# Three attention loops on one core: TensorE's step in a new order, with the product with V right behind the scores

## The chip, the core and the metric

The kernel runs on one core of a Trainium2 chip. The metric is device time in microseconds (us) of one execution, the median of several. The core's engines are TensorE (PE in the rows, with PEld for its weight loads, which overlap its matmuls), VectorE (DVE), ScalarE (ACT), GpSimd (POOL) and SyncE (SP). Each runs its own list of instructions in order, and they meet through semaphores.

## What is computed

The input is x, 128 sequences of 64 tokens with 128 features, and a context of the same shape. Eight layers follow each other, four attentions and four feed-forward layers, each added to x. The change touches the function that computes the attentions of layer 0 (L0a: a mask for each query and key), layer 1 (L1a: a mask for each key, and a relative bias) and the last layer, which the reference calls a feed-forward layer but which is an attention as well (L3f: no mask, projections mixed from four experts for each sequence). In short:

```
for each sequence (64 tokens, 16 heads of 8):
    xhat = layernorm(x)                      # L3f: scaled in the same way
    q = xhat @ Wq; k = ctx @ Wk; v = ctx @ Wv      # L3f: all three from xhat, weights mixed per sequence
    s = q k' * scale + bias (L1a);  s = masked (L0a, L1a)
    p = softmax(s);  o = p @ v
    x = x + o @ Wo + bo
```

## The kernel before

Function `attention` (line 270 on) works on 64 tiles of 128 tokens, two sequences a tile. It is one software pipeline: at step i each engine does, for several tiles at once, one piece each, and `at(i, r, lag)` names tile u = i - lag and its slot s. The order in which these pieces are written out for an engine is the order in which it does them. TensorE's pieces of a step, in the order before the change:

- V (lag 4, lines 464 and 469): the context or xT times Wv, into the bank psQKV.
- masks and scores (lag 4, lines 481 to 500): the relative bias (481, L1a), the masks (493 in tiles of 32x32 of the array in L0a, 488 in L1a), then the scores, 16 matmuls in tiles of 32x64 (500), into psS. They wait for wide_made (GpSimd's product of K with the pattern of heads, line 409).
- TY (lag 1, line 509): the transpose of xhat, into psTY.
- oT (lag 7, line 512): the transpose of the normalised output On, into psO.
- PT0 (lag 5, line 448): four transposes of the first half of the subtracted scores, into psPT.
- QK (lag 2, lines 531 and 533, in L3f 527 with eight matmuls): Q and K, into psQKV.
- O (lag 6, line 543): the exponentials times V, 64 matmuls in tiles of 128x32, into psO.
- Y (lag 7, line 552): oT times Wo, into psTY.
- PT1 (lag 5, line 448): the second four transposes, into psPT again. They wait for pt0_kept, ScalarE's exp that reads the first half.

A float32 matmul here is two instructions, so QK has four loads, V two and Y two; a transpose is one.

ScalarE's pieces, before the change: copy V to Vblk (578 or 583, lag 4); L3f: half of the mixed weights (590); copy oT (597, 601 or 604, lag 7); copy xT (609, lag 1; VectorE does it in L3f, 668); exp of the first half (614, lag 5); copy Q to still and K to flat (624 and 626, 631 and 632, or 634 and 635, lag 2); L3f: the other half of the weights (638); exp of the second half (642, lag 5); L3f: xhat (646).

VectorE's pieces: maximum of the scores (659, lag 4); L3f: copy xT (668); subtraction of the maximum, "less" (674, lag 4); L3f: mixed weights (681); reciprocal and On (690 and 692, lag 6); sum into x (699, lag 7); statistics (703).

Two waits matter. Before V, TensorE waits for `qk_kept` to reach u + 2, which is flat of tile i - 3, copied in ScalarE's step i - 1 (V, Q and K share the bank psQKV); where there are masks, it waits there for `less_made` too, the subtraction of the tile before. That one protects psS, which the masks overwrite:

```python
for u, s in at(i, r, 4):
    wait(pe, qk_kept, u + 2, NT)
    wait(pe, v_kept, u)
    if masked:
        wait(pe, mask_made, u + 1)
        wait(pe, less_made, u)
```

Of the kernel before, what the change touches and what calls it, by code (L numbers as in the profile page):

```python
# [17 lines left out]
P = 128  # L18
# [242 lines left out]
def attention(c, name, sems, w, mask=None, key_mask=False, rel=None, scale=1.0, ctxT=None, q_bias=None, k_bias=None,  # L261
# [6 lines left out]
    with ExitStack() as ctx:  # L268
# [60 lines left out]
        def at(i, r, lag):  # L329

            u = i - lag
            if not isinstance(u, int) or 0 <= u < NT:
                yield u, (r - lag) % RING
# [110 lines left out]
        def _(pe):  # L444
# [7 lines left out]
            def step(i, r):  # L452
# [4 lines left out]
                for u, s in at(i, r, 4):  # L457
                    wait(pe, qk_kept, u + 2, NT)
                    wait(pe, v_kept, u)
                    if masked:  # L460
                        wait(pe, mask_made, u + 1)
                        wait(pe, less_made, u)
                    if not moe:
                        mm = pe.matmul(psQKV[:, 256:384], ctx_sb[:, s, :], w["v"][:, 0, :], start=True, stop=True,
                                       skip_group_check=True)
                    else:
                        for b in range(B2):
                            for h in range(2):
                                mm = pe.matmul(psQKV[S * h:S * h + S, 256 + S * b:256 + S * b + S].rearrange(  # L469
                                    "p (g d) -> p g d", d=DH), xT[:, s, b * S:b * S + S],  # L470
                                               Wc[:, s, b, 2 * P:3 * P].rearrange(
                                                   "k (g h d) -> k g h d", g=8, h=2)[:, :, h, :],
                                               start=b == 0, stop=True, skip_group_check=True)
                    mm.then_inc(v_done, 1)
                for u, s in at(i, r, 4):

                    if not masked:
                        wait(pe, less_made, u)
                    if rel is not None:
                        for g in range(4):  # L480
                            pe.matmul(psS[:, g, 0:256], rel["flip"][:, :],
# [16 lines left out]
                    for g in range(4):  # L498
                        for b in range(B2):
# [2 lines left out]
                                           wide[32 * g:32 * g + 32, s, b].rearrange("p j n -> p (j n)"),  # L502
                                           start=not masked, stop=True, skip_group_check=True)
                    mm.then_inc(s_done, 1)
                for u, s in at(i, r, 1):
                    wait(pe, xhat_made, u + 1)
                    wait(pe, xT_kept, u)
                    wait(pe, x_summed, u - 6)
                    pe.transpose(psTY[:, 0:P], xhat[:, s, :], c.ident[:, :]).then_inc(xT_done, 1)
                for u, s in at(i, r, 7):  # L510
                    wait(pe, on_made, u + 1)
                    pe.transpose(psO[:, ON:ON + P], On[:, s, :], c.ident[:, :]).then_inc(oT_done, 1)  # L512
                for u, s in at(i, r, 5):
                    wait(pe, less_made, u + 1)
                    wait(pe, pt1_kept, u)
                    transposed(u, s, 0).then_inc(pt0_done, 1)
                for u, s in at(i, r, 2):
                    wait(pe, xT_kept, u + 1)
                    wait(pe, qk_kept, u)
# [13 lines left out]
                        mm = pe.matmul(psQKV[:, P:2 * P], w["k"][:, 0, :], ctx_sb[:, s, :], start=False, stop=True,  # L533
                                       skip_group_check=True)
                    mm.then_inc(qk_done, 1)
                for u, s in at(i, r, 6):
                    wait(pe, oT_kept, u)
                    wait(pe, v_kept, u + 1)
                    wait(pe, pt1_kept, u + 1)
                    for gj in range(8):  # L540
                        for q in (0, 2, 1, 3):
                            rows = slice(32 * q, 32 * q + 32)
                            mm = pe.matmul(psO[rows, 18 * gj:18 * gj + 18], PT[:, s % 2, gj, rows],  # L543
                                           Vb[:, s, q // 2, gj].rearrange("p h d -> p (h d)"),
                                           start=gj == 0, stop=True, skip_group_check=True,
                                           tile_position=(0, 32 * q))
                    mm.then_inc(o_done, 1)
                for u, s in at(i, r, 7):
                    wait(pe, oT_kept, u + 1)
                    wait(pe, xT_kept, u + 7, NT)  # L550
                    wait(pe, x_summed, u)
                    pe.matmul(psTY[:, Y:Y + P], oT[:, s, :], w["o"][:, :], start=True, stop=True,  # L552
                              skip_group_check=True).then_inc(y_done, 1)
                for u, s in at(i, r, 5):
                    wait(pe, pt0_kept, u + 1)
                    transposed(u, s, 1).then_inc(pt1_done, 1)
            run_steps(pe, NT, DEPTH, RING, step)

        @block.scalar
        def _(act):  # L560
# [3 lines left out]
            def step(i, r):  # L564
# [22 lines left out]
                if moe:  # L587
                    for u, s in at(i, r, 0):
                        wait(act, wc_made, u - 3)
                        act.activation(Wa[:, s, 0, :], w_all[:, bass.ds(first_at[0], 3 * P)], ACT.Copy,  # L590
                                       scale=moe["two"][:, 0, bass.ds(B2 * u, 1)])
                for u, s in at(i, r, 7):
                    wait(act, oT_done, u + 1)
                    wait(act, y_done, u - 3)
                    if moe:
                        for b in range(B2):
                            last = act.activation(oT[:, s, S * b:S * b + S], psO[:, ON + S * b:ON + S * b + S],  # L597
                                                  ACT.Identity, bias=moe["v_bias"][:, bass.ds(B2 * u + b, 1)])
                        last.then_inc(oT_kept, 1)
                    elif v_bias_col is not None:  # L600
                        act.activation(oT[:, s, :], psO[:, ON:ON + P], ACT.Identity, bias=v_bias_col
                                       ).then_inc(oT_kept, 1)
                    else:
                        act.activation(oT[:, s, :], psO[:, ON:ON + P], ACT.Copy).then_inc(oT_kept, 1)
                if not moe:
                    for u, s in at(i, r, 1):
                        wait(act, xT_done, u + 1)
                        wait(act, qk_done, u - 3)
                        act.activation(xT[:, s, :], psTY[:, 0:P], ACT.Copy).then_inc(xT_kept, 1)
                for u, s in at(i, r, 5):  # L610

                    wait(act, o_done, u - 1)
                    wait(act, pt0_done, u + 1)
                    act.activation(PT[:, s % 2, 0:4, :].rearrange("p g n -> p (g n)"), psPT[:, :], ACT.Exp  # L614
                                   ).then_inc(pt0_kept, 1)
                for u, s in at(i, r, 2):
                    wait(act, qk_done, u + 1)
                    wait(act, s_done, u - 3)
# [32 lines left out]
        def _(dve):  # L651
# [3 lines left out]
            def step(i, r):  # L655
# [29 lines left out]
                        last.then_inc(wc_made, 1)  # L685
                for u, s in at(i, r, 6):
                    wait(dve, o_done, u + 1)
                    wait(dve, oT_done, u - 3)
                    Ov = psO[:, 0:144].rearrange("p (h d) -> p h d", d=DH + 1)
                    dve.reciprocal(rden[:, s, :].unsqueeze(2), Ov[:, :, DH:DH + 1]).then_inc(rden_made, 1)  # L690
                    wait(dve, rden_made, u + 1)
                    dve.tensor_tensor(On[:, s, :].rearrange("p (h d) -> p h d", d=DH), Ov[:, :, 0:DH],  # L692
                                      rden[:, s, :].unsqueeze(2).broadcast_to([P, H, DH]), ALU.mult
                                      ).then_inc(on_made, 1)
# [2110 lines left out]
```

## Time and profile before

| | us |
|---|---|
| median of 3 runs | 2117.54 |
| lowest and highest | 2111.51, 2121.74 |
| span of the profiled execution, first to last instruction | 2107.0 |
| TensorE busy in it (matmul) | 1857.7 (88%) |
| VectorE busy | 1629.4 (77%) |
| ScalarE busy | 1329.5 (63%) |
| GpSimd busy | 1132.4 (54%) |
| L0a, first transpose to last sum into x | 20.7 to 295.5 |
| L1a, the same | 462.8 to 764.8 |
| L3f, the same | 1808.9 to 2104.0 |

For the profiled execution the page gives its span alone, which stands 10.5 under the median of the three runs. In the rows a time is the start from the span's begin, then the duration; "x4" merges four instructions of the same kind, and the duration is then that of the group. The bracket is idle time of the engine just before and what ended it.

### The profile page before, as it was taken

How to read it: one execution, taken by the hardware profiler on the slowest of the kernel's cores; microseconds unless marked ns; L12 is line 12 of the kernel's file. 1: busy time of each engine (PE TensorE's matmuls, PEld its weight loads, DVE VectorE, ACT ScalarE, POOL GpSimd, SP SyncE). 2: the span in 40 equal slices, each digit the busy share in tenths (PEclk: the TensorE clock that was granted, in tenths of full speed). 3: DMA queues.
4: the chain of work that ended last, by engine and by line, in shares of the span. 5: the costliest groups of instructions: out<-in, count | busy, mean ns of one | idle time of the engine just before them, and what ended most of it. 6: DMA issues, size and time to landing. Idle time of an engine off the chain costs nothing. (4 is left out here: it accounts for less than half of the span.)

```text
span 2107.0 us, 79157 instructions
## 1 busy us (share of the span) xinstructions
PE 1857.7 (88%) x31023; PEld 1452.0 (69%) x31023; DVE 1629.4 (77%) x3786; ACT 1329.5 (63%) x3796; POOL 1132.4 (54%) x1424
## 2 busy tenths in 40 slices
PE   5999987979999979999989995899886663799998
PEld 4777754757777758888867763778675442677776
DVE  6888877867777768888856667677555998699998
ACT  4777775656666656666545545556544674699997
POOL 6777744875555525555568873644554243233332
PEclk9999997999999989999999997999998785799999
DMA  5222212001212138000001110135652530000000
GB/s 125 53 53 52 52 39 60 1 18 52 85 52 86 40 58 57 1 1 1 1 25 40 42 29 24 43 132 161 201 199 70 148 96 19 2 19 19 19 19 23
DMA packets 185351, 116.68 MB, mean 55 GB/s; under 512 B 82556, under 2 KB 177432, under 8 KB 181272
## 3 DMA queue, kind: packets, MB, share of 16 engines
q1 hardware_dynamic: 173656, 74.27, 14.7%
q0 software_dynamic: 8064, 35.97, 4.9%
q8 instruction: 252, 4.13, 0.8%
q10 hardware_dynamic: 3264, 1.38, 0.3%
q14 instruction: 115, 0.94, 0.2%
HBM read 83.28 MB, written 28.27 MB: 53 GB/s over the span
## 5 line engine op out<-in xcount | busy, mean ns | idle before, releaser
L1557 POOL TENSOR_TENSOR L1f_hl<-L1f_h,L1f_hh 128x512 fp32r<-128x512 f32 x128 | 167.3, 1308 | 125.6 <-DVE L1f_hh L1569 125.6
L1516 ACT ACTIVATE L1f_h<-L1f_H,L1f_w_b 128x512 f32<-128x512 f32 x192 | 132.4, 690 | 100.8 <-PE L1f_H L969 96.1
L409 POOL TENSOR_TENSOR L3f_wide<-L3f_flat,head_of_row 128x512 f32<-128x512 f32 x64 | 67.2, 1050 | 185.9 <-PE L3f_S L500 167.3
L1569 DVE CAST L1f_hh<-L1f_h 128x512 fp32r<-128x512 f32 x192 | 126.2, 664 | 33.2 <-ACT L1f_h L1516 31.2
L1942 DVE TENSOR_TENSOR L2f_both_h<-L2f_both_G,L2f_both_act 128x512 f32<-128x512 f32 x114 | 78.6, 690 | 94.3 <-ACT L2f_both_act L1917 60.2
L1917 ACT ACTIVATE L2f_both_act<-L2f_both_A 128x512 f32<-128x512 f32 x114 | 68.2, 598 | 122.5 <-PE L2f_both_G L969 88.4
L659 DVE TENSOR_REDUCE L1a_mx<-L1a_S 128x16 f32<-128x1024 f32 x64 | 78.4, 1225 | 75.4 <-PE L1a_S L500 75.4
L409 POOL TENSOR_TENSOR L1a_wide<-L1a_flat,head_of_row 128x512 f32<-128x512 f32 x64 | 66.7, 1042 | 125.1 <-ACT L1a_flat L635 125.1
L1834 POOL DMA_INDIRECT token_y<-L1f_w_w,L2f_both_token x88 | 89.2, 1014 | 76.9 <-DVE L1f_w_w L1961 53.1
L659 DVE TENSOR_REDUCE L0a_mx<-L0a_S 128x16 f32<-128x1024 f32 x64 | 78.3, 1224 | 35.6 <-PE L0a_S L500 35.5
L907 DVE COPY_PREDICATED L2a_weights<-L2a_mask_raw,L2a_S 128x1024 f32<-128x1024 int32 x64 | 86.5, 1352 | 19.8 <-PE L2a_S L824 19.8
L409 POOL TENSOR_TENSOR L0a_wide<-L0a_flat,head_of_row 128x512 f32<-128x512 f32 x64 | 66.6, 1041 | 57.5 <-ACT L0a_flat L632 57.4
L1361 ACT ACTIVATE L0f_parts<-L0f_psA,L0f_w_logits 128x128 f32<-128x128 f32 x256 | 73.2, 369 | 37.7 <-PE L0f_psA L1420 37.7
L659 DVE TENSOR_REDUCE L3f_mx<-L3f_S 128x16 f32<-128x1024 f32 x64 | 78.4, 1224 | 9.7 <-PE L3f_S L500 5.8
L1830 POOL DMA_INDIRECT sorted_x<-L2f_w_xhat_all,L2f_w_place x64 | 67.0, 1047 | 35.0 <-issue 17.1
L1404 DVE SCALAR_TENSOR_TENSOR x_all<-L0f_psD,L0f_w_logits,x_all 128x128 f32<-128x128 f32 x256 | 69.1, 343 | 20.3 <-PE L0f_psD L1420 20.3
L800 POOL TENSOR_TENSOR L2a_wide<-L2a_flat,head_of_row 128x512 f32<-128x512 f32 x64 | 66.6, 1041 | 28.5 <-ACT L2a_still L889 28.5
L674 DVE TENSOR_TENSOR L0a_less_max<-L0a_S,L0a_mx 128x1024 f32<-128x1024 f32 x64 | 78.3, 1224 | 2.2
L674 DVE TENSOR_TENSOR L1a_less_max<-L1a_S,L1a_mx 128x1024 f32<-128x1024 f32 x64 | 78.3, 1224 | 2.2
L448 PE MATMUL L0a_PT<-ident,L0a_less_max 128*128 128x128 f32 x512 | 76.9, 273 | 1.4 <-ACT L0a_probs_T L614 1.4
L448 PE MATMUL L1a_PT<-ident,L1a_less_max 128*128 128x128 f32 x512 | 76.9, 273 | 1.4 <-ACT L1a_probs_T L614 1.4
L642 ACT ACTIVATE L1a_probs_T<-L1a_PT 128x512 f32<-128x512 f32 x64 | 38.3, 598 | 63.0 <-PE L1a_PT L448 63.0
(560 smaller groups left out, 6850.3 us busy)
## 6 DMA issues: line engine op xcount, KB each, us to landing
L0a_mask_raw<-mask SPq DMA_DIRECT2D x256, 32.0 KB, 1.9
expert_split<-L1a_split_halves SPq DMA_DIRECT2D x7, 1152.0 KB, 5.1
L2f_both_xhat<-sorted_x SPq DMA_DIRECT2D x22, 258.0 KB
sorted_x<-L1f_zero SPq DMA_DIRECT2D x4, 1408.0 KB, 21.4
L0a_ctxT<-ctx_T SPq DMA_DIRECT2D x64, 64.0 KB, 1.9
L1a_ctxT<-ctx_T SPq DMA_DIRECT2D x64, 64.0 KB, 1.9
L1a_mask_raw<-mask SPq DMA_DIRECT2D x256, 0.1 KB
L2a_ctxT<-ctx_T SPq DMA_DIRECT2D x64, 64.0 KB, 2.4
```

The costliest lines, as they stand in the source:

```text
L409: pool.tensor_tensor(wide[:, s], flat[:, s, :].rearrange("p (b n) -> p b n", b=B2).unsqueeze(2).broadcast_to([P, B2, 4, S]), c.head_of_row ...
L448: mm = pe.transpose(psPT[:, P * gj:P * gj + P], less[:, s % 2, h:h + 2, :].rearrange("p h k -> p (h k)"), c.ident[:, :])
L659: dve.tensor_reduce(mx[:, s, :].rearrange("p (g j) -> p g j", j=4), S4, AX.X, ALU.max).then_inc(max_made, 1)
L674: dve.tensor_tensor(less[:, s % 2].rearrange("p (g j) k -> p g j k", j=4), S4, mx4.unsqueeze(3).broadcast_to([P, 4, 4, S]), ALU.subtract). ...
L907: dve.copy_predicated(W[:, s].rearrange("p (g j) n -> p g j n", j=4), M_raw[:, s, :].unsqueeze(1).unsqueeze(1).broadcast_to([P, 4, 4, S]), ...
L1361: last = act.activation(parts[:, t % 4, j, :], psA[:, t % 2, j, :], ACT.Copy, scale=c.logits[:, t, HALF + j:HALF + j + 1])
L1404: dve.scalar_tensor_tensor(out=c.x[:, t, :], in0=psD[:, t % 4, e, :], scalar=c.logits[:, t, e:e + 1], in1=c.x[:, t, :], op0=ALU.mult, op1= ...
L1516: act.activation(h[:, q % 3, :], psH[:, q % 2, :], ACT.Relu, bias=b1[:, q:q + 1]).then_inc(h_kept, 1)
L1557: pool.tensor_tensor(hl[:, q % 3, :], h[:, q % 3, :], hh[:, q % 3, :], ALU.subtract).then_inc(hl_pool, 1)
L1569: dve.tensor_copy(hh[:, q % 3, :], h[:, q % 3, :]).then_inc(hh_made, 1)
L1834: pool.indirect_dma_start(r.token_y, bass.IndirectOffsetOnAxis(ap=token[:, g % TR, k:k + 1], axis=0), y_out[:, s, k, :], None).then_inc(y_ ...
L1942: dve.tensor_tensor(h[:, q, :], psG[:, z, :], act_sb[:, q, :], ALU.mult).then_inc(h_made, 1)
```

## The change

On TensorE the step becomes V, masks, scores, O, PT0, oT, TY, QK, PT1, Y. V waits for `less_made` no longer; the masks (or the bias) do. O waits for `on_made` u and for `oT_kept` u - 1 where it waited for `oT_kept` u. On ScalarE the exp of the first half moves ahead of the copies of oT and xT. VectorE's reciprocal waits for `oT_kept` u where it waited for `oT_done` u - 3.

```diff
                 for u, s in at(i, r, 4):
                     wait(pe, qk_kept, u + 2, NT)
                     wait(pe, v_kept, u)
-                    if masked:
-                        wait(pe, mask_made, u + 1)
-                        wait(pe, less_made, u)
...
                 for u, s in at(i, r, 4):
-                    if not masked:
-                        wait(pe, less_made, u)
+                    if masked:
+                        wait(pe, mask_made, u + 1)
+                    wait(pe, less_made, u)
...
                     mm.then_inc(s_done, 1)
+                for u, s in at(i, r, 6):
+                    wait(pe, on_made, u)
+                    wait(pe, oT_kept, u - 1)
+                    wait(pe, v_kept, u + 1)
+                    wait(pe, pt1_kept, u + 1)
+                    for gj in range(8):
...
+                    mm.then_inc(o_done, 1)
+                for u, s in at(i, r, 5):
+                    wait(pe, less_made, u + 1)
+                    wait(pe, pt1_kept, u)
+                    transposed(u, s, 0).then_inc(pt0_done, 1)
+                for u, s in at(i, r, 7):
+                    wait(pe, on_made, u + 1)
+                    pe.transpose(psO[:, ON:ON + P], On[:, s, :], c.ident[:, :]).then_inc(oT_done, 1)
                 for u, s in at(i, r, 1):
...
                     pe.transpose(psTY[:, 0:P], xhat[:, s, :], c.ident[:, :]).then_inc(xT_done, 1)
-                for u, s in at(i, r, 7):
...
-                for u, s in at(i, r, 5):
-                    wait(pe, less_made, u + 1)
-                    wait(pe, pt1_kept, u)
-                    transposed(u, s, 0).then_inc(pt0_done, 1)
                 for u, s in at(i, r, 2):
...
                     mm.then_inc(qk_done, 1)
-                for u, s in at(i, r, 6):
-                    wait(pe, oT_kept, u)
-                    wait(pe, v_kept, u + 1)
-                    wait(pe, pt1_kept, u + 1)
...
+                for u, s in at(i, r, 5):
+                    wait(pe, pt0_kept, u + 1)
+                    transposed(u, s, 1).then_inc(pt1_done, 1)
                 for u, s in at(i, r, 7):
                     wait(pe, oT_kept, u + 1)
                     wait(pe, xT_kept, u + 7, NT)
...
-                for u, s in at(i, r, 5):
-                    wait(pe, pt0_kept, u + 1)
-                    transposed(u, s, 1).then_inc(pt1_done, 1)

         def _(act):
...
+                for u, s in at(i, r, 5):
+                    wait(act, o_done, u - 1)
+                    wait(act, pt0_done, u + 1)
+                    act.activation(PT[:, s % 2, 0:4, :].rearrange("p g n -> p (g n)"), psPT[:, :], ACT.Exp
+                                   ).then_inc(pt0_kept, 1)
                 for u, s in at(i, r, 7):
                     wait(act, oT_done, u + 1)
...
-                for u, s in at(i, r, 5):
-
-                    wait(act, o_done, u - 1)
-                    wait(act, pt0_done, u + 1)
-                    act.activation(PT[:, s % 2, 0:4, :].rearrange("p g n -> p (g n)"), psPT[:, :], ACT.Exp
-                                   ).then_inc(pt0_kept, 1)

         def _(dve):
...
                 for u, s in at(i, r, 6):
                     wait(dve, o_done, u + 1)
-                    wait(dve, oT_done, u - 3)
+                    wait(dve, oT_kept, u)
```

## Rows read from the trace of the kernel before

**Rows 1.** Busy time by engine (PE, PEld, DVE, ACT, POOL), then clock, DMA.

```profile
30.00:45.00 15.00, 12.86 (x312) 9.38 (x313) 13.80 (x37) 11.17 (x34) 12.19 (x18) 1.00 0.20 48
```

**Rows 2.** Timeline of one steady step of L0a: start, duration, engine, line.

```profile
153.21 0.30 PEld L464 LDWEIGHTS L0a_QKV<-L0a_w_v,L0a_ctxT 128*128 128x128 f32 x2 [0.17 <-issue]
...
153.63 0.14 PEld L493 LDWEIGHTS L0a_S<-L0a_mask_bias,ident_bf 32*32 32x32 bf16 x16
...
153.89 0.23 PEld L500 LDWEIGHTS L0a_S<-L0a_wide,L0a_still 32*64 32x64 f32 x16
...
154.50 0.14 PEld L509 LDWEIGHTS L0a_TY<-ident,L0a_xhat 128*128 128x128 f32 x1 [0.39 <-POOL L0a_xhat L418]
...
154.67 0.47 PEld L448 LDWEIGHTS L0a_PT<-ident,L0a_less_max 128*128 128x128 f32 x4
...
155.11 0.30 PEld L531 LDWEIGHTS L0a_QKV<-L0a_xT,L0a_w_q 128*128 128x128 f32 x2
...
155.48 0.60 ACT L614 ACTIVATE L0a_probs_T<-L0a_PT 128x512 f32<-128x512 f32 x1
155.76 0.64 PEld L543 LDWEIGHTS L0a_O<-L0a_Vblk,L0a_probs_T 128*32 128x32 f32 x64
...
155.94 1.23 DVE L674 TENSOR_TENSOR L0a_less_max<-L0a_S,L0a_mx 128x1024 f32<-128x1024 f32 x1
...
156.22 0.37 ACT L632 ACTIVATE L0a_flat<-L0a_QKV,L0a_w_bk 128x128 f32<-128x128 f32 x1
156.43 0.30 PEld L552 LDWEIGHTS L0a_TY<-L0a_w_o,L0a_oT 128*128 128x128 f32 x2
...
156.64 0.47 PEld L448 LDWEIGHTS L0a_PT<-ident,L0a_less_max 128*128 128x128 f32 x4
...
157.28 0.30 PEld L464 LDWEIGHTS L0a_QKV<-L0a_w_v,L0a_ctxT 128*128 128x128 f32 x2 [0.17 <-issue]
...
157.39 0.60 ACT L642 ACTIVATE L0a_probs_T<-L0a_PT 128x512 f32<-128x512 f32 x1 [0.80 <-PE L0a_PT L448]
```

**Rows 3.** Timeline of L0a's last steps, where O waited for ScalarE's oT copy.

```profile
292.32 0.36 ACT L601 ACTIVATE L0a_oT<-L0a_O,L0a_w_bv 128x128 f32<-128x128 f32 x1
292.73 0.64 PEld L543 LDWEIGHTS L0a_O<-L0a_Vblk,L0a_probs_T 128*32 128x32 f32 x64 [1.04 <-ACT L0a_oT L601]
```

**Rows 4.** Timeline of one steady step of L1a.

```profile
600.68 0.30 PEld L464 LDWEIGHTS L1a_QKV<-L1a_w_v,L1a_ctxT 128*128 128x128 f32 x2 [0.17 <-issue]
...
602.41 0.14 PEld L509 LDWEIGHTS L1a_TY<-ident,L1a_xhat 128*128 128x128 f32 x1 [0.39 <-issue]
...
602.88 0.28 ACT L604 ACTIVATE L1a_oT<-L1a_O 128x128 f32<-128x128 f32 x1 [0.68 <-PE L1a_O L512]
...
603.06 0.27 ACT L609 ACTIVATE L1a_xT<-L1a_TY 128x128 f32<-128x128 f32 x1
...
603.38 0.60 ACT L614 ACTIVATE L1a_probs_T<-L1a_PT 128x512 f32<-128x512 f32 x1
...
604.03 0.28 ACT L635 ACTIVATE L1a_flat<-L1a_QKV 128x128 f32<-128x128 f32 x1
...
605.18 0.30 PEld L464 LDWEIGHTS L1a_QKV<-L1a_w_v,L1a_ctxT 128*128 128x128 f32 x2 [0.17 <-issue]
```

**Rows 5.** L3f: VectorE's xT copies from 1850 us on (durations, first and last start), then timeline.

```profile
L668 DVE COPY L3f_xT<-L3f_TY x53: 279/281/281, 1850.1 to 2078.3; 128x128 f32<-128x128 f32 x53
...
1938.58 0.33 ACT L624 ACTIVATE L3f_still<-L3f_QKV,L3f_w_q_bias 128x64 f32<-128x64 f32 x1
...
1939.37 0.66 ACT L638 ACTIVATE L3f_weights_first<-L3f_w_all,L3f_w_two 128x384 f32 x1
1939.93 0.60 ACT L642 ACTIVATE L3f_probs_T<-L3f_PT 128x512 f32<-128x512 f32 x1
...
2082.22 0.97 PEld L527 LDWEIGHTS L3f_QKV<-L3f_xT,L3f_weights_both 128*128 128x128 f32 x8
...
2083.37 0.31 ACT L624 ACTIVATE L3f_still<-L3f_QKV,L3f_w_q_bias 128x64 f32<-128x64 f32 x1 [0.18 <-PE L3f_QKV L527]
```

More of the change, by code:

```diff
@@ L504, in step @@
                     mm.then_inc(s_done, 1)
+                for u, s in at(i, r, 6):
[4 more added lines that the diff above has]
+                    for gj in range(8):
+                        for q in (0, 2, 1, 3):
+                            rows = slice(32 * q, 32 * q + 32)
+                            mm = pe.matmul(psO[rows, 18 * gj:18 * gj + 18], PT[:, s % 2, gj, rows],
+                                           Vb[:, s, q // 2, gj].rearrange("p h d -> p (h d)"),
+                                           start=gj == 0, stop=True, skip_group_check=True,
+                                           tile_position=(0, 32 * q))
+                    mm.then_inc(o_done, 1)
[6 more added lines that the diff above has]
+                    pe.transpose(psO[:, ON:ON + P], On[:, s, :], c.ident[:, :]).then_inc(oT_done, 1)
                 for u, s in at(i, r, 1):
@@ L509, in step @@
                     pe.transpose(psTY[:, 0:P], xhat[:, s, :], c.ident[:, :]).then_inc(xT_done, 1)
-                for u, s in at(i, r, 7):
-                    wait(pe, on_made, u + 1)
-                    pe.transpose(psO[:, ON:ON + P], On[:, s, :], c.ident[:, :]).then_inc(oT_done, 1)
-                for u, s in at(i, r, 5):
-                    wait(pe, less_made, u + 1)
-                    wait(pe, pt1_kept, u)
-                    transposed(u, s, 0).then_inc(pt0_done, 1)
                 for u, s in at(i, r, 2):
@@ L535, in step @@
                     mm.then_inc(qk_done, 1)
-                for u, s in at(i, r, 6):
-                    wait(pe, oT_kept, u)
-                    wait(pe, v_kept, u + 1)
-                    wait(pe, pt1_kept, u + 1)
[L540 to L547, printed above, removed]
+                for u, s in at(i, r, 5):
+                    wait(pe, pt0_kept, u + 1)
+                    transposed(u, s, 1).then_inc(pt1_done, 1)
                 for u, s in at(i, r, 7):
```

## The prediction

> **What bounds the kernel now.** I read busy time and granted clock by stretches first (TensorE leads in all three attentions), then the timeline of a steady step of each, then the places where an engine visibly waited, for the hand-overs. All three attentions (L0a, L1a, L3f) are loops of 64 tiles over five in-order engines. In L0a TensorE works without a hole: its loads follow each other from V at 153.21 to the next V at 157.28, 4.07 us a step [rows 2]. The reader should look at load starts, since the next load is what a wait holds back. Between full-array operations the starts are 0.11 us apart (PT0's four loads take 154.67 to 155.11). One hole stands out: the second transposes start at 156.64, so V could load at 156.64 + 0.44 = 157.08, and it loads at 157.28. The subtraction (less, line 674) ends at 155.94 + 1.23 = 157.17, and V waits for it: 0.11 us of hand-over from VectorE. So L0a has a second loop as long as TensorE's own: scores, maximum, subtraction, V, masks, scores. L1a is the same with 4.50 us, 600.68 to 605.18 [rows 4]. In L3f V never waited for less; there the steps are 4.39 us, (2078.3 - 1850.1)/52 [rows 5], shared by ScalarE, VectorE and TensorE.
>
> **The change, part by part.** Positions below count from PT0's first load, "t".
>
> 1. V no longer waits for less. Alone that is worth the hole, 157.28 - 157.08 = 0.20 us a step in L0a and, with the same 2.77 us between the load after the scores and V [rows 4], in L1a; nothing in L3f.
>
> 2. O (64 loads and matmuls in 128x32 tiles) moves behind the scores. It used to stand between QK and Y. QK to O is 155.76 - 155.11 = 0.65 us, and QK has only four loads of 0.11, so 0.21 of this is the change of tile size [rows 2]. That goes. O itself stays 156.43 - 155.76 = 0.67. The scores to the next load stay 154.50 - 153.89 = 0.61, whoever is next. TensorE's own sum is then V and masks and scores 154.50 - 153.21 = 1.29, O 0.67, PT0 0.44, oT 0.11, TY 0.11, QK 0.44, PT1 0.44, Y 0.22: 3.72 us against 4.07. In L1a the first term is 602.41 - 600.68 = 1.73, and the sum 4.16 against 4.50.
>
> 3. The distance from PT0 to PT1 shrinks from 1.97 us (154.67 to 156.64, [rows 2]) to 0.44 + 0.11 + 0.11 + 0.44 = 1.10, and both use one PSUM bank. PT1 waits for the first exp (pt0_kept). An exp starts 157.39 - 156.64 = 0.75 after its first load when ScalarE is idle and takes 0.60 [rows 2]; ScalarE's result reaches TensorE 0.05 later (292.32 + 0.36 = 292.68, O loads at 292.73) [rows 3]. PT1 can load at t + 1.40: TensorE now waits 0.30 there, and V does not escape it. So 0.30 of the 0.35 is given back at once.
>
> 4. The first exp moves ahead of the copies of oT and xT on ScalarE, and still and flat (the copies of Q and K) stay behind all three. V of the next step waits for flat (qk_kept), and this is what becomes late. Today flat is done at 156.22 + 0.37 = 156.59, 0.69 before V [rows 2]. After the change the chain is: exp starts t + 0.75; exp and still take 156.22 - 155.48 = 0.74 between them until flat could start; oT and xT are now in front too. In L1a the oT copy lasts 0.28 and the next starts 0.18 behind it [rows 4], so a copy occupies its duration less 0.10: oT 0.36 - 0.10 = 0.26, xT 0.18. Flat takes 0.37. The next V loads at t + 0.75 + 0.74 + 0.26 + 0.18 + 0.37 + 0.05 = t + 2.35. TensorE, held by PT1, would have been there at 1.40 + 0.44 + 0.22 = 2.06. From V it is 1.29 + 0.67 = 1.96 to the next PT0, because O now stands in this part of the loop: **L0a 4.31 us a step, 0.24 more.** QK has landed by then: its four loads start at t + 0.66.
>
> 5. L1a has shorter copies (no bias): exp and still until flat 604.03 - 603.38 = 0.65, oT 0.18, xT 0.18, flat 0.28 [rows 4]. V loads at t + 0.75 + 1.29 + 0.05 = 2.09; + 1.73 + 0.67 = **4.49, 0.01 less than now.**
>
> 6. L3f's QK has eight loads, and ScalarE builds half of the mixed weights. QK loads at t + 0.66; still starts 2083.37 - 2082.22 = 1.15 after that where it waits [rows 5], t + 1.81. Four copies until the second weights take 1939.37 - 1938.58 = 0.79, weights until the second exp 0.56, the exp 0.60, then 0.05, and O may load (it waits for pt1_kept, and stands early in the next step now); 0.67 later PT0: 1.81 + 0.79 + 0.56 + 0.60 + 0.05 + 0.67 = **4.48 against 4.39, 0.09 more.** TensorE there is no limit: PT1 comes at 0.44 + 0.22 + 0.88 = 1.54, behind 1.40. VectorE copies xT between maximum and subtraction; TY comes 0.67 + 0.44 + 0.11 = 1.22 later behind the scores than before, and the maximum that runs meanwhile is an instruction of the size of the subtraction, 1.23 [rows 2]. I take nothing, and keep it for the upper end.
>
> 7. Waits with one answer. VectorE's reciprocal now waits for this step's oT copy; behind it are On, the sum into x and the statistics. The copy ends at t + 0.75 + 0.48 + 0.36 = 1.59 (still, as long as oT, takes 0.26 of the 0.74, the exp 0.48), the subtraction ahead of it at t - 1.28 + (157.17 - 153.89) = 2.00, so it is hidden by 0.41. O's new waits (on_made, oT_kept of earlier tiles) ask for work of the step before. Y waits for this step's xT copy: t + 1.23 + 0.26 + 0.27 + 0.05 = 1.81 (0.27 is the duration in [rows 4]) against PT1's end of loads at 1.84: nothing, by a hair. No DMA is moved; POOL's wide follows flat, and its scores are two steps on.
>
> V and O both run in 58 of the steps. **Sum: 58 x (0.24 - 0.01 + 0.09) = 18.6 us.** The profiled span is 2107.0 us, which becomes 2125.6. It lies 10.5 under the median of the three runs, 2117.5, what lies around the span being in that; the difference carried over gives **2136 us**.
>
> Bounds. Above: if xT holds ScalarE for its whole 0.27 (+0.09), if the hand-over costs VectorE's 0.11 and not 0.05 (+0.06), and if the weights hold ScalarE 0.66 and not 0.56, the three stages come to 58 x (0.39 + 0.14 + 0.25) = 45 us; all of these at once is unlikely, and I take half of what is above my sum: 2150. Below: 0.05 a step less in each stage, as the starts are read to 0.01 and eight are added: 2128.
>
> **Rivals.**
> A. *TensorE's own order decides* and the exps and copies are hidden. L0a 3.72 (-0.35). L1a is then held by the old loop without V, 4.50 - 0.22 = 4.28 (-0.22). L3f stays. 58 x -0.57 = -33: 2084. For it: four changes of tile size a step where there were five, each with a hole in the loads. Against: PT1 would have to follow PT0 in 1.10 with a 0.60 exp that starts at 0.75. The Trainium skill, "TensorEngine Tiling (Array Packing)", Key Properties, says that changing the tiling mode drains the TensorE; the holes in the loads agree, and by that rule alone the change is a gain of one drain a step.
>
> B. *O's loads slip under the scores* (the other side). The sixteen loads of the scores end 0.23 after the first; if O's loads could start there and not at 0.61, 0.38 goes in L0a (4.31 to 3.93, -0.14) and L1a (4.49 to 4.11, held at 4.28, -0.22); L3f's loop does not contain the scores (+0.09). 58 x -0.27 = -16: 2102. It decides from about 0.24 of overlap. Against: the masks' loads end 0.14 after 153.63 and the scores' first load is at 153.89, 0.12 later, so between two small tile sizes nothing slipped [rows 2]. The Trainium skill, "TensorE: Matmul & The Clock Gate", Part 2, says that the queue pulls weight loads ahead of running matmuls if row groups don't conflict or the background weights are the target; by it the time would be B's, and the masks' row speaks against it.
>
> C. *V is not held by flat*, only PT1 by the exp: 3.72 + 0.30 = 4.02 in L0a (-0.05), 4.46 in L1a (-0.04), L3f level. 58 x -0.09 = -5: 2112. It needs ScalarE to finish flat 0.29 earlier than my chain.
>
> D. *The clock.* TensorE would be idle 4.31 - 3.72 = 0.59 us in each step of L0a, 14%. If that took the granted clock to 0.9 in all three stages, about 2.4 us of each loop would grow by a tenth: + 42, 2178. Against: from 30 to 45 us TensorE was busy 12.86 of 15.00 us, also 14% idle, at a clock of 1.00 [rows 1].
>
> **How the numbers follow.** My forecast 0.65, A 0.05, B 0.10, C 0.13, D 0.07. Half a percent, 10.6 us, is about what a measurement of this kernel can tell from none: slower from 2128. Slower: D and my forecast less 0.06 of its low side, 0.66. Same: C, that 0.06 and 0.02 of B, 0.21. Faster: A and the rest of B, 0.13. The forecast's own range is 2128 to 2150; the whole one goes down to B and keeps a little above: 2102 to 2154.
>
> **What would show it.** In L0a and L1a: the wait ahead of V put down to ScalarE's flat, about 0.3 us a step in L0a and next to none in L1a, and a wait ahead of PT1 put down to the first exp, about 0.3. V at 2.35 behind PT0 in L0a. The scores' load to O's 0.61. In L3f the wait ahead of O, put down to the second exp. Steps of 4.31, 4.49, 4.48. The prediction is wrong if O loads sooner than 0.4 behind the scores, or V follows Y without a hole, or the clock in these stages is below 1.00.

## The result and the profile after

The changed kernel takes 2140.48 us (median of 4 runs, 2137.24 to 2148.47) against 2117.64 for the one before (4 runs): 1.0118 times as long, 95% interval 1.0093 to 1.0143. It is slower by 22.8 us. Predicted were 2136 us and 18.6 us more. A second set of runs (e5 below) gave 1.0144, 1.0127 to 1.0161. So the side and about the size of the loss came out as predicted, but one of the three stages loses more than twice what I gave it.

The profiled execution is the longest of the four runs, 2148.47 us at a span of 2146.7, so 1.8 us lie around the span. The page begins:

```profile
span 2146.7 us, 79350 instructions
PE 1860.9 (87%) x31023; PEld 1454.2 (68%) x31023; DVE 1635.6 (76%) x3786; ACT 1320.1 (61%) x3796; POOL 1131.2 (53%) x1424
```

Busy times are those of before within 10 us (TensorE 1857.7): nothing was added, so the time went into waits. From its first transpose to its last sum into x, L0a now takes 20.4 to 310.7 (15.5 us longer than before), L1a 477.4 to 778.7 (0.7 shorter) and L3f 1833.2 to 2143.7 (15.4 longer). That is 30 of the 39.7 us between the two spans. Of the rest 8.0 us fall on L2f, a stage that the change does not touch (355.2 us from its first to its last matmul before, 363.2 after). The medians, 22.8 us apart, leave no room for them. The purest measure of the loops is the time from a stage's first maximum to its last, 63 steps:

| | before | after | difference | predicted, 58 steps |
|---|---|---|---|---|
| L0a | 258.8 (27.5 to 286.3) | 272.5 (27.5 to 300.0) | +13.7 | +13.9 |
| L1a | 285.5 (470.5 to 756.0) | 283.7 (484.9 to 768.6) | -1.8 | -0.6 |
| L3f | 274.2 (1820.0 to 2094.2) | 288.8 (1844.3 to 2133.1) | +14.6 | +5.2 |

**L0a.** The timeline of a steady step of L0a in the changed kernel (start, duration, engine, line, operation):

```profile
152.96 0.64 PEld L511 LDWEIGHTS L0a_O<-L0a_Vblk,L0a_probs_T 128*32 128x32 f32 x64 [0.39 <-issue]
...
153.62 0.42 PEld L448 LDWEIGHTS L0a_PT<-ident,L0a_less_max 128*128 128x128 f32 x4
...
154.38 0.60 ACT L594 ACTIVATE L0a_probs_T<-L0a_PT 128x512 f32<-128x512 f32 x1 [1.26 <-PE L0a_PT L448]
...
154.88 0.36 ACT L605 ACTIVATE L0a_oT<-L0a_O,L0a_w_bv 128x128 f32<-128x128 f32 x1
155.03 0.42 PEld L448 LDWEIGHTS L0a_PT<-ident,L0a_less_max 128*128 128x128 f32 x4 [0.27 <-ACT L0a_probs_T L594]
...
155.12 0.28 ACT L613 ACTIVATE L0a_xT<-L0a_TY 128x128 f32<-128x128 f32 x1
155.28 0.38 ACT L629 ACTIVATE L0a_still<-L0a_QKV,L0a_w_bq_scaled 128x128 f32<-128x128 f32 x1
155.53 0.39 ACT L630 ACTIVATE L0a_flat<-L0a_QKV,L0a_w_bk 128x128 f32<-128x128 f32 x1
...
155.97 0.30 PEld L461 LDWEIGHTS L0a_QKV<-L0a_w_v,L0a_ctxT 128*128 128x128 f32 x2 [0.20 <-ACT L0a_flat L630]
...
156.65 0.23 PEld L498 LDWEIGHTS L0a_S<-L0a_wide,L0a_still 32*64 32x64 f32 x16
...
157.27 0.64 PEld L511 LDWEIGHTS L0a_O<-L0a_Vblk,L0a_probs_T 128*32 128x32 f32 x64 [0.39 <-issue]
```

Follow it from PT0 at 153.62. Its exp starts 0.76 later and ends at 154.98, and PT1 loads at 155.03. ScalarE goes on without a hole through oT, xT, still and flat. Flat ends at 155.53 + 0.39 = 155.92 and V loads at 155.97, that is 2.35 behind PT0. The bracket counts the idle time of the load unit alone, 0.27 ahead of PT1 and 0.20 ahead of V. Counted by load starts, as the prediction does, PT1 could have loaded at 154.67, 0.22 behind K's first load at 154.45, and V at 155.69, 0.22 behind Y's at 155.47: TensorE is held 0.36 and 0.28. The step is 157.27 - 152.96 = 4.31 us, against 4.07 in [rows 2]. The list of waits for 60 to 280 us (engine, what waited, what for: total us, times, longest) shows that nearly every step is like this one:

```profile
PEld L0a_O L511 <- issue: 19.6, 51, 0.4
PEld L0a_PT L448 <- ACT L0a_probs_T L594: 13.1, 48, 0.3
PEld L0a_QKV L461 <- ACT L0a_flat L630: 10.2, 50, 0.2
```

**L1a.** The same places of a step there. No wait is listed ahead of V, but it loads 0.05 behind the end of flat (622.42 + 0.31 = 622.73), as in L0a, and 0.29 behind Y's first load at 622.49 where 0.22 would do. So flat holds it, by 0.07 us. The step is 624.51 - 620.03 = 4.48 us against 4.50 in [rows 4]:

```profile
620.03 0.64 PEld L511 LDWEIGHTS L1a_O<-L1a_Vblk,L1a_probs_T 128*32 128x32 f32 x64 [0.39 <-issue]
...
622.42 0.31 ACT L633 ACTIVATE L1a_flat<-L1a_QKV 128x128 f32<-128x128 f32 x1
...
622.78 0.30 PEld L461 LDWEIGHTS L1a_QKV<-L1a_w_v,L1a_ctxT 128*128 128x128 f32 x2
...
624.51 0.64 PEld L511 LDWEIGHTS L1a_O<-L1a_Vblk,L1a_probs_T 128*32 128x32 f32 x64 [0.39 <-issue]
```

**L3f.** Here O waits, but not for the second exp. From the timeline of a step:

```profile
1985.55 0.64 PEld L511 LDWEIGHTS L3f_O<-L3f_Vblk,L3f_probs_T 128*32 128x32 f32 x64 [0.59 <-DVE L3f_On L690]
...
1986.22 0.42 PEld L448 LDWEIGHTS L3f_PT<-ident,L3f_less_max 128*128 128x128 f32 x4
...
1986.72 0.14 PEld L527 LDWEIGHTS L3f_TY<-ident,L3f_xhat 128*128 128x128 f32 x1
...
1987.14 0.29 DVE L666 COPY L3f_xT<-L3f_TY 128x128 f32<-128x128 f32 x1 [0.31 <-PE L3f_TY L527]
1987.34 1.22 DVE L672 TENSOR_TENSOR L3f_less_max<-L3f_S,L3f_mx 128x1024 f32<-128x1024 f32 x1
...
1988.47 1.14 DVE L679 SCALAR_TENSOR_TENSOR L3f_weights_both<-L3f_w_all,L3f_w_two,L3f_weights_first 128x384 f32<-128x384 f32 x2
...
1988.96 0.31 PEld L466 LDWEIGHTS L3f_QKV<-L3f_weights_both,L3f_xT 128*64 128x64 f32 x8 [0.54 <-ACT L3f_flat L624]
...
1989.29 0.61 ACT L640 ACTIVATE L3f_probs_T<-L3f_PT 128x512 f32<-128x512 f32 x1
...
1989.82 0.29 DVE L690 TENSOR_TENSOR L3f_On<-L3f_O,L3f_rden 128x128 f32<-128x128 f32 x1
...
1990.16 0.64 PEld L511 LDWEIGHTS L3f_O<-L3f_Vblk,L3f_probs_T 128*32 128x32 f32 x64 [0.58 <-DVE L3f_On L690]
```

The loop goes O, PT0, oT, TY on TensorE, then xT, less, mixed weights, reciprocal and On on VectorE, then the next O: 4.61 us. VectorE stops 0.31 for TY, and TY stands behind O. The second exp ends at 1989.90 and would have let O load at 1989.95, 0.21 sooner. The waits from 1870 to 2100 us:

```profile
PEld L3f_O L511 <- DVE L3f_On L690: 29.0, 50, 0.6
...
DVE L3f_xT L666 <- PE L3f_TY L527: 15.3, 50, 0.4
```

By stretches, the granted clock (the number before the DMA share) is 1.00, the upper of its two levels (2.4 GHz), in all three attentions, with TensorE busy 97, 98 and 90% of them:

```profile
60.00:280.00 220.00, 213.00 (x5803) 159.39 (x5797) 174.91 (x312) 147.50 (x505) 152.42 (x203) 1.00 0.21 50
500.00:740.00 240.00, 234.02 (x5624) 188.10 (x5622) 181.20 (x320) 142.20 (x533) 128.30 (x195) 1.00 0.20 67
1870.00:2100.00 230.00, 206.02 (x5395) 169.07 (x5384) 212.88 (x399) 217.19 (x651) 72.75 (x100) 1.00 0.07 19
```

### The profile page after: what moved, and what is told of

It reads as the page before. It is cut to its first block and busy times, and to the rows that moved or that the text cites. A ratio compares the mean times of both kernels' runs of the same rounds, so it can differ in the third digit from the quotient of the medians.

```text
span 2146.7 us, 79350 instructions
## 1 busy us (share of the span) xinstructions
PE 1860.9 (87%) x31023; PEld 1454.2 (68%) x31023; DVE 1635.6 (76%) x3786; ACT 1320.1 (61%) x3796; POOL 1131.2 (53%) x1424
## 5 line engine op out<-in xcount | busy, mean ns | idle before, releaser
L594 ACT ACTIVATE L1a_probs_T<-L1a_PT 128x512 f32<-128x512 f32 x64 | 38.2, 597 | 110.1 <-PE L1a_PT L448 110.1
L905 DVE COPY_PREDICATED L2a_weights<-L2a_mask_raw,L2a_S 128x1024 f32<-128x1024 int32 x64 | 86.5, 1351 | 15.5 <-PE L2a_S L822 15.5
L448 PE MATMUL L1a_PT<-ident,L1a_less_max 128*128 128x128 f32 x512 | 84.4, 286 | 8.8 <-ACT L1a_probs_T L594 2.5
L448 PE MATMUL L0a_PT<-ident,L0a_less_max 128*128 128x128 f32 x512 | 83.9, 286 | 9.0 <-ACT L0a_probs_T L594 2.9
L594 ACT ACTIVATE L0a_probs_T<-L0a_PT 128x512 f32<-128x512 f32 x64 | 38.2, 597 | 81.3 <-PE L0a_PT L448 81.3
L448 PE MATMUL L3f_PT<-ident,L3f_less_max 128*128 128x128 f32 x512 | 80.9, 281 | 1.9 <-ACT L3f_probs_T L594 1.9
```

The lines of the kernel that those rows point to most:

```text
L448: mm = pe.transpose(psPT[:, P * gj:P * gj + P], less[:, s % 2, h:h + 2, :].rearrange("p h k -> p (h k)"), c.ident[:, :])
L905: dve.copy_predicated(W[:, s].rearrange("p (g j) n -> p g j n", j=4), M_raw[:, s, :].unsqueeze(1).unsqueeze(1).broadcast_to([P, 4, 4, S]), ...
```

## The experiments

Eight kernels ran, on two chips: e1 to e4 on one, where the kernel before took 2108.21 us, e5 to e8 on another, where it took 2078.66. Times are compared by ratio to the kernel before on the same chip, steps and stages by the traces. "First to last maximum" is the measure of the table above. The step lengths are medians over a stage. The 4.39 of L3f before is a mean; its median was 4.35, and the mean after is 4.61.

### e1: the kernel before, V freed of the subtraction

```diff
                 for u, s in at(i, r, 4):
                     wait(pe, qk_kept, u + 2, NT)
                     wait(pe, v_kept, u)
-                    if masked:
-                        wait(pe, mask_made, u + 1)
-                        wait(pe, less_made, u)
...
                 for u, s in at(i, r, 4):
-                    if not masked:
-                        wait(pe, less_made, u)
+                    if masked:
+                        wait(pe, mask_made, u + 1)
+                    wait(pe, less_made, u)
```

> The kernel before with one part of the change: V does not wait for the subtracted scores, the masks and the bias do. Theory (the 0.20 us hole ahead of V was VectorE's subtraction): the hole closes in L0a and L1a, steps 3.87 and 4.30 us, L3f level, 58 x 0.40 = 23 us less, 2094 us. Rival (the hole belongs to TensorE's own sequence, since the trace put it down to nothing): steps of 4.07 and 4.50 as before, 2118 us.

Measured: 2093.33 us, ratio 0.9932 (0.9913 to 0.9951), 15 us less; steps 3.92 in L0a, 4.31 in L1a, L3f as before. First to last maximum: L0a 255.2 (-3.6), L1a 274.5 (-11.0), L3f 273.8 (-0.4). No wait ahead of V is listed any more, where the kernel before has 49 in 60 to 280 us. From the timeline, the loads of PT1 and of the next V:

```profile
155.12 0.47 PEld L448 LDWEIGHTS L0a_PT<-ident,L0a_less_max 128*128 128x128 f32 x4
155.56 0.30 PEld L461 LDWEIGHTS L0a_QKV<-L0a_w_v,L0a_ctxT 128*128 128x128 f32 x2
```

So this half of the change is a gain, and the loss comes from the rest. The profile of before put the hole ahead of V down to "issue" [rows 2]. Freeing V of VectorE's subtraction closed it, so it was that wait. The edit takes the wait for the mask from V as well, but in steady steps of the kernel before GpSimd's last mask was done at least 1.36 us before V in L0a and 3.08 in L1a, the subtraction 0.12 (median of both). L1a gave 11.0 of the 11.6 us that 0.20 a step makes. L0a gave only 3.6, 8.0 short. Its median step is 0.05 longer than expected, which is 2.9 us over 58. Most of the rest is single long steps: from 40 to 290 us, by the starts of the maximum, 11 steps are more than 0.3 over the median (up to 5.06), 7.1 us together. In the kernel before they are 3 steps and 1.6 us, in the changed one 4 steps and 2.6 us. In long ones TensorE stops in the middle of its work. Here it is within the 64 loads of O; in another step it is 1.27 us between the masks' loads and the scores':

```profile
101.40 0.26 PEld L541 LDWEIGHTS L0a_O<-L0a_Vblk,L0a_probs_T 128*32 128x32 f32 x18
...
102.24 0.14 PEld L541 LDWEIGHTS L0a_O<-L0a_Vblk,L0a_probs_T 128*32 128x32 f32 x4 [0.58 <-issue]
```

The 64 matmuls of O have no wait among them. What stops TensorE there, and why e1 has more such steps, stays open.

### e2: e1, with O alone moved behind the scores

ScalarE's order and the places of PT0 and Y stay as before. O and the reciprocal have the waits of the changed kernel.

```diff
                     mm.then_inc(s_done, 1)
+                for u, s in at(i, r, 6):
+                    wait(pe, on_made, u)
+                    wait(pe, oT_kept, u - 1)
...
+                    mm.then_inc(o_done, 1)
                 for u, s in at(i, r, 1):
...
                     mm.then_inc(qk_done, 1)
-                for u, s in at(i, r, 6):
-                    wait(pe, oT_kept, u)
...
-                    mm.then_inc(o_done, 1)
...
                     wait(dve, o_done, u + 1)
-                    wait(dve, oT_done, u - 3)
+                    wait(dve, oT_kept, u)
```

> The kernel before with V freed of the subtraction and O moved behind the scores, but PT0 still behind TY and oT, Y still ahead of PT1, and ScalarE's order as before. Theory (what costs in L0a is the copies that stand between the first exp and V): flat is done 1.91 us after PT0's first load, V 0.05 later, then 1.29 + 0.67 + 0.22 to the next PT0: L0a 4.14 us a step, L1a 4.51, L3f 4.48, 2125 us. Rival (O's place alone costs what the change costs): L0a 4.31, 2140 us. Rival (fewer changes of tile size pay once ScalarE's order is left alone): L0a 3.9, L1a 4.3, under 2110 us.

Measured: 2118.39 us, ratio 1.0053 (1.0033 to 1.0073); steps 4.10, 4.41 and 4.47; first to last maximum 260.4, 279.6 and 281.8, that is 5.2, 5.1 and 8.0 above e1. From the waits from 60 to 280 us, then from the timeline of a step of L3f:

```profile
PEld L0a_PT L448 <- ACT L0a_probs_T L613: 12.5, 51, 0.2
```

```profile
1987.36 0.61 ACT L641 ACTIVATE L3f_probs_T<-L3f_PT 128x512 f32<-128x512 f32 x1
...
1987.55 0.29 DVE L691 TENSOR_TENSOR L3f_On<-L3f_O,L3f_rden 128x128 f32<-128x128 f32 x1
...
1988.08 0.66 PEld L511 LDWEIGHTS L3f_O<-L3f_Vblk,L3f_probs_T 128*32 128x32 f32 x64 [0.44 <-DVE L3f_On L691]
```

O's place alone takes back what e1 gained, and more. It joins O to the scores, which saves one change of array tile size. But with O gone from between PT0 and PT1 the two come as close as in the changed kernel, and meet over their one bank, and PT1 waits 0.24 for the first exp. In L0a V is held as well: it loads 0.05 behind flat in nearly every step, 0.08 later than PT1 alone would let it, with ScalarE's order still the old one. The theory was right to 0.04 in L0a and 0.01 in L3f; L1a is 0.10 shorter than it said.

In L3f the profile names On for O's wait, but On ends at 1987.84, 0.24 before O loads, and O loads 0.67 behind the scores' first load at 1987.41, just as in e4 and e6, where On is done 0.96 us or more before O. So On does not hold O here; V, 0.05 behind flat, is what the step shares with those two. TY stands 0.69 behind O in this kernel and VectorE does not wait for it. In the changed kernel TY stands 1.17 behind O (1985.55 to 1986.72), behind PT0 and oT, and VectorE waits. So it is the rest of the new order that brings On into the loop. This is read from the two timelines; no run moves TY alone.

From e2 to the changed kernel (PT0 right behind O, oT ahead of TY, PT1 ahead of Y, the exp in front on ScalarE) the stages grow by another 12.1, 4.1 and 7.0 us by first to last maximum. The medians split the loss otherwise: in per cent of the kernel before, e1 is at -0.68, e2 at +0.53 and the changed kernel at +1.18, so O's move has 1.21 and the rest 0.65.

### e3: the changed kernel, the first exp behind the copies of oT and xT again

```diff
-                for u, s in at(i, r, 5):
-                    wait(act, o_done, u - 1)
-                    wait(act, pt0_done, u + 1)
-                    act.activation(PT[:, s % 2, 0:4, :].rearrange("p g n -> p (g n)"), psPT[:, :], ACT.Exp
-                                   ).then_inc(pt0_kept, 1)
                 for u, s in at(i, r, 7):
...
                         act.activation(xT[:, s, :], psTY[:, 0:P], ACT.Copy).then_inc(xT_kept, 1)
+                for u, s in at(i, r, 5):
+                    wait(act, o_done, u - 1)
+                    wait(act, pt0_done, u + 1)
+                    act.activation(PT[:, s % 2, 0:4, :].rearrange("p g n -> p (g n)"), psPT[:, :], ACT.Exp
+                                   ).then_inc(pt0_kept, 1)
```

> The changed kernel with ScalarE's first exp put back behind the copies of oT and xT. Theory (with PT1 close behind PT0 the exp is urgent): the exp starts 1.31 us after PT0's first load and not 0.75, PT1 at 1.96; L0a 4.58 us a step, L1a 4.94, L3f unchanged, 42 us more than the changed kernel, 2182 us. Rival (it is the exp's place ahead of the copies that makes flat late, and V with it): V is served sooner, steps at or below 4.2 in L0a, 2125 us or less.

Measured: 2171.29 us, ratio 1.0295 (1.0271 to 1.0319); first to last maximum L0a 286.8 (14.3 above the changed kernel), L1a 302.0 (+18.3), L3f 288.7 (level); steps 4.45, 4.81 and 4.61, where the theory had 4.58 and 4.94 in L0a and L1a. A step of L0a:

```profile
150.47 0.42 PEld L448 LDWEIGHTS L0a_PT<-ident,L0a_less_max 128*128 128x128 f32 x4
...
151.69 0.60 ACT L612 ACTIVATE L0a_probs_T<-L0a_PT 128x512 f32<-128x512 f32 x1
...
152.34 0.42 PEld L448 LDWEIGHTS L0a_PT<-ident,L0a_less_max 128*128 128x128 f32 x4 [0.74 <-ACT L0a_probs_T L612]
```

With the exp last of the three, PT1 waits 0.74 instead of 0.27. So the exp's early place is no cause of the loss. It is what TensorE's new order needs, and without it the kernel would be 3% slower than before. The size was a little too high: the exp came at t + 1.22 and PT1 at t + 1.87, not 1.31 and 1.96. The rival had one thing right: V is no longer held by flat, which ends 0.14 before it. But PT1 is later by more than that gives.

### e4: the changed kernel, in L3f the reciprocal and On ahead of VectorE's mixed weights

```diff
-                if moe:
-                    for u, s in at(i, r, 1):
-                        wait(dve, wa_made, u + 1)
...
-                        last.then_inc(wc_made, 1)
                 for u, s in at(i, r, 6):
                     wait(dve, o_done, u + 1)
                     wait(dve, oT_kept, u)
...
+                if moe:
+                    for u, s in at(i, r, 1):
+                        wait(dve, wa_made, u + 1)
...
+                        last.then_inc(wc_made, 1)
```

> The changed kernel with VectorE's reciprocal and On ahead of the mixed weights in L3f. Theory (L3f's steps of 4.61 us are a loop in which O waits for On of the tile before, and On stands behind the weights, 1.06 us): O is next held by the second exp, steps 4.40 us in L3f, 58 x 0.21 = 12 us less than the changed kernel, 2128 us. Rival (VectorE has no time left in the step wherever On stands): 4.61 as it was, 2140 us. L0a and L1a are as in the changed kernel under both.

Measured: 2130.27 us, ratio 1.0107 (1.0083 to 1.0130). L3f's step is 4.48 and its first to last maximum 280.5, 8.3 below the changed kernel. Waits from 1860 to 2090 us:

```profile
PEld L3f_QKV L466 <- ACT L3f_flat L624: 27.7, 51, 0.5
PEld L3f_O L511 <- issue: 22.3, 51, 0.4
...
DVE L3f_xT L666 <- PE L3f_TY L527: 9.7, 50, 0.3
```

O's wait for On is gone, and the rest is what O shows behind the scores in every stage. It is done 0.96 before O now, where it was 0.05 before. So On behind the mixed weights was what set L3f's step, worth 0.13 of the 0.22 us. This rests on the trace: the ratio, 1.0107, is not clear of the changed kernel's 1.0118. Expected were 4.40 and 12 us. Something else stands at 4.48, and e6 asks whether it is VectorE's remaining wait for TY.

### e5: the changed kernel once more, beside the next three

> The changed kernel once more, on the chip of these four runs, as their yardstick. Both theories: 1.012 of the kernel before, steps of 4.31, 4.48 and 4.61 us in L0a, L1a and L3f.

Measured: 2106.62 us, ratio 1.0144 (1.0127 to 1.0161); steps 4.31, 4.48 and 4.61; first to last maximum 271.1, 283.2 and 288.2. The loss is there on this chip too.

### e6: e4, with VectorE's xT copy behind the subtraction in L3f

```diff
-                if moe:
-                    for u, s in at(i, r, 1):
...
-                        wait(dve, xT_done, u + 1)
-                        wait(dve, v_done, u - 3)
-                        dve.tensor_copy(xT[:, s, :], psTY[:, 0:P]).then_inc(xT_kept, 1)
                 for u, s in at(i, r, 4):
                     wait(dve, max_made, u + 1)
...
                                       ).then_inc(less_made, 1)
+                if moe:
+                    for u, s in at(i, r, 1):
...
+                        wait(dve, xT_done, u + 1)
+                        wait(dve, v_done, u - 3)
+                        dve.tensor_copy(xT[:, s, :], psTY[:, 0:P]).then_inc(xT_kept, 1)
```

> The changed kernel with both moves on VectorE in L3f: On ahead of the mixed weights, and the copy of xT behind the subtraction. Theory (with On first, steps of 4.48 us are VectorE's own list and its wait for TY, 0.18 us ahead of xT): the wait goes, the second exp holds O, 4.40 us a step, 58 x 0.21 = 12 us less than the changed kernel. Rival (the steps of 4.48 are ScalarE's and TensorE's loop already): 4.48, 8 us less than the changed kernel.

Measured: 2105.13 us, ratio 1.0131 (1.0114 to 1.0148); L3f's step is 4.48 again, first to last maximum 281.5. VectorE no longer waits for TY at all, and the step has not moved. The median is only 1.5 us below e5's, where L3f gives 6.7; in the profiled executions L2f, which no edit touches, is 9.5 us longer than in e5. So the loop that is left is ScalarE's and TensorE's, as the rival had it. The timeline, from PT0 to PT0:

```profile
1970.46 0.42 PEld L448 LDWEIGHTS L3f_PT<-ident,L3f_less_max 128*128 128x128 f32 x4
...
1972.82 0.33 ACT L624 ACTIVATE L3f_flat<-L3f_QKV,L3f_w_k_bias 128x64 f32<-128x64 f32 x1
...
1973.20 0.31 PEld L466 LDWEIGHTS L3f_QKV<-L3f_weights_both,L3f_xT 128*64 128x64 f32 x8 [0.25 <-ACT L3f_flat L624]
1973.52 0.61 ACT L640 ACTIVATE L3f_probs_T<-L3f_PT 128x512 f32<-128x512 f32 x1
...
1974.25 0.66 PEld L511 LDWEIGHTS L3f_O<-L3f_Vblk,L3f_probs_T 128*32 128x32 f32 x64 [0.44 <-issue]
...
1974.94 0.42 PEld L448 LDWEIGHTS L3f_PT<-ident,L3f_less_max 128*128 128x128 f32 x4
```

QK's result is copied in four pieces, the last flat ends at 1973.15, and V loads at 1973.20. From V it is 1.05 to O and 0.69 to PT0: 2.74 + 1.05 + 0.69 = 4.48. The second exp would let O go at 1974.13 + 0.05 = 1974.18, 0.07 before it went. O also loads 0.67 behind the scores' first load, where L0a and L1a have 0.62 in every run with the new place of O. So two chains, V behind flat and the second exp, end here almost together, each 0.05 to 0.07 short of O, and the runs do not settle which of them holds it. My 4.40 had taken 0.99 and 0.67 for the last two, from the changed kernel. Why they are 0.08 longer stays open.

### e7: the changed kernel with one more ScalarE copy in L0a and L1a

A copy of 128x128 whose result nobody reads is put in front of still. It computes nothing that is needed.

```diff
+                if not moe:
+                    for u, s in at(i, r, 2):
+                        act.activation(idle_copy[:, s, :], c.ident[:, :], ACT.Copy)
                 for u, s in at(i, r, 2):
                     wait(act, qk_done, u + 1)
```

> The changed kernel with one more instruction on ScalarE in L0a and L1a, a copy of a constant 128x128 ahead of still, which nobody uses. Theory (V is held by flat in the changed order): each step grows by what such a copy occupies, 0.18 us by its kind, to 4.49 in L0a and 4.66 in L1a, 21 us in all. Rival (TensorE's own list is the bound and flat has room): 4.31 and 4.48 as without it.

Measured: 2130.87 us in one run, 24 above e5; steps 4.51, 4.67 and 4.61, so 0.20, 0.19 and 0 more. First to last maximum 282.9 (+11.8), 294.2 (+11.0), 288.0. In L0a's timeline:

```profile
150.97 0.32 ACT L617 ACTIVATE L0a_idle_copy<-ident 128x128 f32<-128x128 f32 x1
...
151.42 0.39 ACT L634 ACTIVATE L0a_flat<-L0a_QKV,L0a_w_bk 128x128 f32<-128x128 f32 x1
...
151.86 0.30 PEld L462 LDWEIGHTS L0a_QKV<-L0a_w_v,L0a_ctxT 128*128 128x128 f32 x2 [0.40 <-ACT L0a_flat L634]
```

The copy holds ScalarE for 0.20, and the whole of it comes out in the step. V's wait goes from 0.20 to 0.40. ScalarE's list from the first exp to flat is on the loop in both stages.

### e8: the same copy in e1, TensorE's old order

> The same extra copy in the old order with V freed of the subtraction (the kernel of e1). Theory (there flat is done 0.4 us before V even in the shorter step): no change, 3.92 us in L0a and 4.32 in L1a. Rival (ScalarE's list holds TensorE in either order): 0.18 a step more here too.

Measured: 2058.92 us in one run, against 2078.66 for the kernel before. Steps 3.91, 4.31 and 4.38 and first to last maximum 255.1 and 274.5 in L0a and L1a, as in e1 without the copy (255.2 and 274.5). Flat and V of a step of L0a:

```profile
153.68 0.37 ACT L634 ACTIVATE L0a_flat<-L0a_QKV,L0a_w_bk 128x128 f32<-128x128 f32 x1
...
154.38 0.30 PEld L462 LDWEIGHTS L0a_QKV<-L0a_w_v,L0a_ctxT 128*128 128x128 f32 x2
```

Flat is done 0.33 before V (0.53 in e1), so the same 0.20 us costs nothing in the old order. There O stands between QK and the next V and gives ScalarE the time. With e7 this shows that it is the new order that makes V late, not ScalarE's amount of work. The changed kernel differs from e1 in ScalarE's order as well, but in e2, which has ScalarE's old one, V in L0a is already held by flat.

## Why the prediction was right, and where it was not

**The drain and TensorE's own sum (parts 1 and 2).** The scores' load to O's is 156.65 to 157.27 = 0.62, and O to PT0 0.66, against 0.61 and 0.67 in the sum. So O's loads do not slip under the scores, and rival B is out. The Trainium skill, "TensorE: Matmul & The Clock Gate", Part 2, has weight loads pulled ahead of running matmuls if row groups don't conflict or the background weights are the target. Across these two tile sizes the trace shows no such pull: the load unit stands idle 0.39 us ahead of O. Whether one of the two conditions held here, no run shows. One change of tile size less in each step did not shorten it either: the step grew. By the Trainium skill, "TensorEngine Tiling (Array Packing)", Key Properties, each change of tiling mode drains the engine. The traces agree that a hole exists (QK's first load to O's was 0.65 us before, 0.21 more than its four loads), but what it saves is only worth something where TensorE sets the step.

**PT1 behind the exp (part 3).** PT1 at t + 1.41, predicted 1.40. By load starts it is held 0.36, predicted 0.30. Rival A, in which PT1 is not held, is out, and e3 shows that this wait grows with whatever is put in front of the exp.

**V behind flat in L0a (part 4).** V at t + 2.35, a step of 4.31, both as predicted. Rival C said that V is not held by flat. The wait for flat is there in 50 steps, and e7 and e8 make it a loop rather than a coincidence. By load starts V is held 0.28 (the profile's idle time is 0.20), predicted "about 0.3".

**L1a (part 5).** 4.48, predicted 4.49; V at t + 2.08, predicted 2.09, with next to no wait, as predicted. e7's copy lengthened this step by 0.19 all the same, so TensorE and ScalarE were level, flat ahead of it by 0.07.

**L3f (parts 6 and 7): the step that failed.** I gave it 0.09 and it took 0.22 us a step. The sentence that failed is in part 7, "O's new waits (on_made, oT_kept of earlier tiles) ask for work of the step before", costed at nothing. On of the tile before is work of the step before in L0a and L1a, where VectorE is done with it at 156.11, 1.16 before O. In L3f it stands on VectorE behind 1.14 us of mixed weights, and O now comes 0.67 before PT0 instead of after QK, with TY 1.17 behind O. Beside it, part 6 took nothing for VectorE's xT waiting for TY. It waits 0.31 of each step, and that lies in the same loop. The size of 4.48 that I gave for ScalarE's chain is what e2, e4 and e6 measured (4.47, 4.48, 4.48) with On out of the way. There V's wait for flat and the second exp, which the prediction named, end within 0.02 us of each other, and which of them holds O stays open.

**The clock (rival D).** 1.00 in all three stages, as the windows above show, so rival D is out.

**The sum.** By first to last maximum it is 13.7 - 1.8 + 14.6 = 26.5 us against my 18.6. The medians differ by 22.8 and in e5's set by 28.0. That 2136 is only 4.5 us off is in part luck: the median of 4 runs shows less than the traces do, and less than e5's set. The prediction took the 10.5 between span and median for what lies around the span. In the changed kernel that is 1.8 us. If it was so before as well, the other 8.7 are a profiled execution that was shorter than the median one. A sum of differences is not hurt by that.

**Which half costs what**, by first to last maximum over the three stages: V freed of the subtraction -15.0 (e1), O moved +18.3 (e2 against e1), the rest of the new order +23.2 (changed kernel against e2, on different chips; L0a is 11.0 and not 12.1 us longer if e4, on e2's chip, stands for it). By medians the three are -0.68, +1.21 and +0.65%. In both counts only the first part is a gain, and e1 is faster than both kernels, 0.9932 of the one before.

## What to carry to other kernels

Before operations are regrouped by array tile size, count for each shared bank how far its first use is from its second, and put the consumer's in-order list of work between them. Here the two transposes stood 0.87 us closer in TensorE's own list and the next V could not come closer to the copy that frees its bank, and in L0a two saved holes of about 0.2 us were paid for with 0.36 and 0.28 us in which TensorE was held. A wait that an operation does not itself need (the subtraction ahead of V) can be moved to the one that does for free; it was the only part that paid. And when an operation is moved forward, look where each thing it waits for stands on its engine in every stage that shares the code: one stage of three had 1.14 us of other work in front. Where a profile names one engine for a wait on several semaphores, compare the end of that instruction with the start of the waiting one: in e2's L3f the one named had ended 0.24 us before.

## What the runs showed that was not expected

- A hole that the profile puts down to "issue" can be a wait on a semaphore, and a wait that it puts down to an engine (On in e2's L3f) can be another. The one ahead of V closed in e1 once VectorE's subtraction was no longer asked for.
- TensorE stops for 0.6 to 1.3 us among small loads in some steps of L0a, with nothing that the trace shows it waiting for. In e1 such steps took back 5.5 us (7.1 - 1.6) of the 11.6 expected of that stage. The cause is open.
- The level differs between sets of runs (the kernel before took 2117.64, 2108.21 and 2078.66 us in the three, the last two on different chips), while the changed kernel's ratio was 1.0118 and 1.0144, with intervals that overlap. In the kept traces the difference lies in L2f, which no edit touches: from its first to its last matmul it takes 352 to 363 us in the first pair and in e1 to e4, and 319 to 330 us in e5 to e8. Why is open.
- A ScalarE copy of 128x128 occupies the engine for less than its duration: xT 0.16 of 0.28, oT 0.24 of 0.36, the extra copy 0.20 of 0.32.
